# One token slot of a ViT tower on TensorE, its instruction order changed: scores together, turns together, fold and turned p later

## The chip, the cores and the metric

The kernel runs on one core of a Trainium2 chip. The metric is device time in microseconds (us), the median of several runs of the same program, lower is better. One more execution was recorded by the hardware profiler; its span, its busy times and its rows below come from that execution.

The engines are named as in the profile: PE is TensorE's matmul, PEld its weight load, DVE is VectorE, ACT is ScalarE, POOL is GpSimd, SP is SyncE, which issues most DMAs. Each engine runs its own instructions strictly in the written order and waits on semaphores.

## What is computed

A tower of three parts over 32 images of 256 x 64 x 64 (float32), cut to what matters:

```python
# tokenizer: 4x4 patches, one query per patch (the patch mean), keys and values from its 16 pixels
q    = LN(patch_mean) @ Wq.T
k, v = LN(pixels) @ Wkv.T
attn = softmax(q * scale . k)            # 8 heads, 16 pixels
h    = patch_mean + (attn . v) @ proj_w.T + proj_b
h    = concat([cls_tok, h])
# layer: a recurrence over the images (32 steps), then 8 experts, top 2
h = h + scan(tanh(LN(h) @ W_ih.T + b + hidden @ W_hh.T))
h = h + moe(LN(h))
```

## The kernel before, in words

The 8192 patches are worked in 64 units of 128 patches. `over_slots` (L91) writes out 66 slots, one after the other, without a loop on the chip. In slot k five units are in work at once: unit u = k is fetched and normalised (`front`), v = k-1 gets its attention scores and softmax (`mid`), w = k-2 its values and projection (`back`), z = k-3 the recurrence (`end`), and unit k-4 its routing (`late`). 61 slots, k = 3 to 63, have both `front` and `end`. After the slots come 86 expert tiles and the gather of the results, which the change does not touch.

Every engine has a function `slot` with its own written order; that order is what the change edits. Each helper is a few instructions with its waits ahead of it. On PE (L1040 to L1088), with the shape of the stationary tile (rows x columns of the array):

- 128x32: `means` (L883, patch means of u), `score` in two halves (L931, unit v), `fold_patches` (L948, v), `values` (L986, w).
- 128x128: `turn_z` 0 to 3 (L978, transposes of w), `turn_rn` (L897, u), `turn_xn` (L1005, z), `queries` (L904, u), `turn_tok` (L335), `recur` (L1013, z, float16), `turn_p` (L956, v), `project_out` (L998, w), `turn_h` (L1033, z), `logits` (L348), `turn_rs` (L925, u).
- 32x128: `project` (L913, u). 64x32: `weigh` (L961, v).

What joins the engines around the change:

- `means` of u; ACT `mean_out` writes rT (L725); DVE `mean_stats` (L1154), POOL `mean_scale` (L638), DVE `mean_norm` writes rn (L1169); PE `turn_rn`; ACT `rn_out` writes rnT; PE `queries`; ACT `q_out` writes qT (L736); PE `project`; ACT `u_out` (L744, four passes).
- `score` of v; DVE `unmask` writes sm (L1174); PE `fold_patches`; DVE `logits_in` (L1177, three steps); ACT `exps` (L756); DVE `total` and `divide`, which writes pr (L1198); PE `turn_p`; DVE `spread_p` writes pd (L1206); PE `weigh`.
- DVE `token_norm` writes xn of z (L1229); PE `turn_xn`; ACT `xn_out`; DVE `token_low` (L1232); PE `recur`; ACT `hidden` (L793); PE `turn_h`.
- `turn_z` of w; ACT `zT_out`; PE `values`; ACT `a_out`; PE `project_out`; DVE `token_stats`.
- DVE `stats` 0 to 7 of u, then `pixel_var` (L1148); POOL `pixel_scale` (L651); PE `turn_rs`; ACT `rep_out`; the next slot's `score`.

On SP the loads of pixels for unit k+2 go out in four parts of xp and four of xc, each behind a semaphore of PE (L577 to L606); `clear_rows` (L568) writes zeros behind `fold_patches`. xp has 4 buffers, xc has 3. From slot 43 on (`scatter_now`, L111) POOL also scatters two routed rows in each of 16 slots.

Of the kernel before, what the change touches and what calls it, by code (L numbers as in the profile page):

```python
# [72 lines left out]
def wait(eng, sem, unit, per, plus):  # L73

    v = unit.count(per, plus)
    if isinstance(v, int) and v <= 0:
        return
    eng.wait_ge(sem, v)
# [38 lines left out]
def vit_tower(nc, xc_in, xp_in, cls_tok, ln_q_w, ln_q_b, wqT, ln_kv_w, ln_kv_w_col, ln_kv_b, wk, wvT, projT, proj_b,  # L117
# [6 lines left out]
    with ctx:  # L124
# [123 lines left out]
        s = {n: sem(n) for n in names}  # L248
# [290 lines left out]
        @block.sync  # L539
        def _(sp):  # L540
            row_of = lambda a, n: a.partition_broadcast(n)
            for dst, src in ((spread[:, :], spread_in), (ident[:, :], ident_in)):
                sp.dma_start(dst, src).then_inc(s["first_in"], 16)
            load_xp(sp, 0, 0)
            loads = [(own[:, :], own_in), (cls_row[:, :], row_of(cls_tok, B)),
                     (fold[:, :], fold_in), (pick[:, :], pick_in),
                     (bih_c[:, :], b_ih), (bhh_c[:, :], b_hh),
                     (raw_ih, wihT.rearrange("(c p) n -> p c n", p=P)),
                     (raw_hh, whhT.rearrange("(c p) n -> p c n", p=P)),
                     (rw_s[:, :, :], routerT.rearrange("(c p) e -> p c e", p=P)),  # L550
                     (iota8[:, :], iota_in), (tri32, tri_in), (tile_no[:, :], tile_in[:, 0:NT]),
                     (before8[:, :, :], before_in.rearrange("p (a b) -> p a b", b=E))]
            assert len(loads) == NCONST
            for dst, src in loads:
                sp.dma_start(dst, src).then_inc(s["consts_in"], 16)
            sp.dma_start(b1_s[:, :, :], b1.rearrange("p (e c) -> p e c", e=E)).then_inc(s["consts_in"], 16)
            load_xc(sp, 0, 0)
            load_xp(sp, 1, 1)
            sp.wait_ge(s["w_ready"], 2)
            sp.wait_ge(s["rec_w"], 3)  # L560
            load_xc(sp, 1, 1)
            load_xp(sp, 2, 2)
            load_xc(sp, 2, 2)
            load_xp(sp, 3, 3)
            pieces = [(g, q, min(q + 3, 2 * TILES[g])) for g in GROUPS for q in range(0, 2 * TILES[g], 3)]
            sp.wait_ge(s["zero_set"], 1)

            def clear_rows(sp, n):  # L568

                g, q, e = pieces[n]  # L570
                sp.dma_start(xs_dram[g][q * P:e * P, :].rearrange("(k p) r -> p k r", p=P),
                             zero[:, :].unsqueeze(1).to_broadcast([P, e - q, C])).then_inc(clear[g], 16)

            def slot(sp, u, front, mid, back, end, late):
                v, w, t = u.before(), u.before(2), u.k - 4
                more_xp, more_xc = back and w.k + XBUF < UNITS, mid and v.k + XC < UNITS
                if more_xp:  # L577
                    wait(sp, s["z_ps"], w, 2, 2)
                    load_xp(sp, w.x, w.k + XBUF, [0])
                    wait(sp, s["rT_ps"], u, 1, 1)  # L580
                    load_xp(sp, w.x, w.k + XBUF, [1])
                    wait(sp, s["zt_ps"], w, 4, 2)
                    load_xp(sp, w.x, w.k + XBUF, [2])
                    wait(sp, s["rn_ps"], u, 1, 1)
                    load_xp(sp, w.x, w.k + XBUF, [3])
                for q in scatter_now(u.k)[1:]:
                    load_row(sp, q)
                if mid and 0 <= u.k - 2 < len(pieces):
                    wait(sp, s["c_ps"], v, 1, 1)
                    clear_rows(sp, u.k - 2)  # L590
                if more_xc:
                    wait(sp, s["s_ps"], v, 1, 1)
                    wait(sp, s["q_ps"], u, 1, 1)
                    load_xc(sp, v.c, v.k + XC, [0])
                if late:
                    keep_base(sp, t)
                    keep_row(sp, t)
                if more_xc:
                    if back:
                        wait(sp, s["a_ps"], w, 1, 1)  # L600
                    load_xc(sp, v.c, v.k + XC, [1])
                    wait(sp, s["u_ps"], u, 1, 1)
                    load_xc(sp, v.c, v.k + XC, [2])
                    if back:
                        wait(sp, s["pj_ps"], w, 1, 1)
                    load_xc(sp, v.c, v.k + XC, [3])  # L606
                for q in scatter_now(u.k + 1)[:1]:
                    load_row(sp, q)
                if u.k == UNITS - 1:
                    sp.wait_ge(s["s_ps"], UNITS - 2)  # L610
                    for e in range(E):
                        sp.dma_start(w1_in_s[:, e, :, :], w1[e].rearrange("(c p) n -> p c n", p=P)).then_inc(w1_in, 16)
                if u.k == UNITS:
                    sp.wait_ge(s["s_ps"], UNITS - 1)
                    for e in range(E):
                        sp.dma_start(w2_in_s[:, e, :, :], w2[e].rearrange("(c p) n -> p c n", p=P)).then_inc(w2_in, 16)
                if u.k == UNITS + 2:
                    sp.wait_ge(s["s_ps"], UNITS)
                    for q in range(RX):
                        sp.wait_ge(sent[q], 32 * len(range(q, SIZES[0], RX)))  # L620
                    for k in range(AHEAD):
                        load_tile(sp, 0, k, k)

            over_slots(sp, slot)
# [81 lines left out]
        def _(act):  # L706
# [107 lines left out]
            def slot(act, u, front, mid, back, end, late):  # L814
                v, w, z = u.before(), u.before(2), u.before(3)
# [8 lines left out]
                if back:  # L824
                    zT_out(act, w, 2)
                    zT_out(act, w, 3)
                if mid:
                    exps(act, v)
                if front:
                    q_out(act, u)  # L830
                if end:
                    xn_out(act, z)
                if back:
                    a_out(act, w)
                if front:
# [45 lines left out]
        def _(pe):  # L881
# [158 lines left out]
            def slot(pe, u, front, mid, back, end, late):  # L1040
                v, w, z = u.before(), u.before(2), u.before(3)
                if front:
                    means(pe, u)
                if mid:
                    score(pe, v, 0)
                if back:
                    turn_z(pe, w, 0)
                    turn_z(pe, w, 1)
                if mid:
                    score(pe, v, 1)  # L1050
                if back:
                    turn_z(pe, w, 2)
                if front:
                    turn_rn(pe, u)
                if back:
                    turn_z(pe, w, 3)
                if mid:
                    fold_patches(pe, v)
                if end:
                    turn_xn(pe, z)  # L1060
                if front:
                    queries(pe, u)
                if back:
                    values(pe, w)
                if front:
                    project(pe, u, back)
                if mid:
                    turn_p(pe, v)
                if late:
                    turn_tok(pe, u.k - 4, FB)  # L1070
                if end:
                    recur(pe, z, 0)
                    recur(pe, z, 1)
                if back:
                    project_out(pe, w)
                if end:
                    turn_h(pe, z)
                if late:
                    logits(pe, u.k - 4, FB)
                for g, part in pieces_now(u.k):  # L1080
                    if part == 4:
                        pe.wait_ge(s["lg_done"], u.k - 3)
                        route_ranks(pe, g, FB)
                if mid:
                    weigh(pe, v, front, 0)
                    weigh(pe, v, front, 1)
                if front:
                    turn_rs(pe, u)  # L1088
# [42 lines left out]
        def _(dve):  # L1131
# [128 lines left out]
            def slot(dve, u, front, mid, back, end, late):  # L1260
                v, w, z = u.before(), u.before(2), u.before(3)
# [12 lines left out]
                    route_norm(dve, u.k - 4)  # L1274
                if front:
                    stats(dve, u, [5])
                if mid:
                    logits_in(dve, v)
                if front:
                    stats(dve, u, [6])  # L1280
                if mid:
                    total(dve, v)
                    divide(dve, v)
                if end:
                    token_low(dve, z)
                if front:
                    stats(dve, u, [7])
                    pixel_var(dve, u)
                if mid:
                    spread_p(dve, v)  # L1290
# [408 lines left out]
```

## Time and profile before

| what | value |
|---|---|
| median of 3 runs | 1481.64 us (1477.16 to 1483.23) |
| span of the profiled execution | 1542.8 us |
| its PE, PEld, DVE, ACT, POOL busy | 87%, 69%, 69%, 54%, 46% |
| token slots (first to last `means`) | about 13 to 1095 us of the span |

For the profiled execution no time is listed besides its span; the span is 61 us (4%) above the median of the runs, so differences worked out inside the profile are taken off the median as they are. Busy is the time between an instruction's start and its modelled end; matmuls overlap, so the start of one group to the start of the next is what a group costs on PE. A bracket behind a row, as [0.25 <-ACT qT L736], is idle time ahead of it and what ended that idle time.

### The profile page before, as it was taken

To read this page: it belongs to the slowest core of one execution; us is meant where nothing else is said; L and a number is where in the kernel's file an instruction comes from. 1 tells how busy PE (TensorE), PEld (TensorE's weight loads), DVE (VectorE), ACT (ScalarE), POOL (GpSimd) and SP (SyncE) were. 2 spreads that over 40 slices of the span, in tenths; PEclk is the share of its full clock that TensorE was granted. 3 is DMA by queue.
4 is the path that set the end of the run, shared out by engine and by line. 5 is a ranking of instruction groups with operands and counts; after the bars stand their busy time and mean duration, and the time that the engine had idled before them with its cause. 6 is when DMAs were issued, how large, how long until landed. Compare 5 with 4: busy or idle time off the path is not lost. (4 is left out here: it accounts for less than half of the span.)

```text
span 1542.8 us, 63164 instructions
## 1 busy us (share of the span) xinstructions
PE 1342.3 (87%) x25681; PEld 1061.8 (69%) x25681; DVE 1067.5 (69%) x2855; ACT 832.4 (54%) x2065; POOL 711.1 (46%) x854
## 2 busy tenths in 40 slices
PE   4899999999999999999999999999959997688670
PEld 3677777777777777777776776677748896467550
DVE  4677777777777777878666666678756764467464
ACT  1455665655655655555555555555647774355340
POOL 2243343444434434343555555553313777552555
PEclk9999999999999999999999999999989998799795
DMA  7998898988998998988888989897245887687677
GB/s 259 407 307 298 293 308 297 305 295 295 310 297 276 314 293 280 294 278 293 303 309 302 300 306 312 296 313 256 71 153 193 272 283 245 186 267 255 207 232 227
DMA packets 186620, 423.78 MB, mean 275 GB/s; under 512 B 23968, under 2 KB 89312, under 8 KB 186208
## 3 DMA queue, kind: packets, MB, share of 16 engines
q1 hardware_dynamic: 170336, 380.27, 73.2%
q0 software_dynamic: 14048, 38.16, 7.8%
q8 instruction: 209, 3.42, 0.9%
q10 hardware_dynamic: 1952, 1.32, 0.3%
q14 instruction: 75, 0.61, 0.1%
HBM read 332.26 MB, written 87.39 MB: 272 GB/s over the span
## 5 line engine op out<-in xcount | busy, mean ns | idle before, releaser
L1146 DVE BATCH_NORM_STATS2 st<-xp 128x6 f32<-128x512 f32 x512 | 339.8, 695 | 16.4 <-DMA xp<-xpix 16.0
L656 POOL TENSOR_TENSOR rs_px<-px_ve,half_neg 128x16 f32<-128x16 f32 x64 | 187.0, 2922 | 179.9 <-DVE px_ve L1151 179.9
L770 ACT ACTIVATE zT<-bank 128x512 f32<-128x512 f32 x256 | 138.7, 597 | 75.3 <-PE bank L983 75.2
L1465 POOL DMA_INDIRECT y<-ys_dram,slot x130 | 126.3, 971 | 112.5 <-DVE fin L1628 47.1
L641 POOL TENSOR_TENSOR q_rs<-q_ve,half_neg 128x1 f32<-128x1 f32 x64 | 35.1, 549 | 289.7 <-DVE q_ve L1163 289.7
L763 ACT ACTIVATE z_s<-bank 128x512 f32<-128x512 f32 x256 | 138.6, 597 | 49.0 <-PE bank L973 49.0
L942 PE MATMUL bank<-xc,u 128*32 128x64 f32 x8192 | 149.4, 220 | 17.6 <-issue 17.0
L942 PEld LDWEIGHTS bank<-xc,u 128*32 128x32 f32 x8192 | 132.1, 110 | 41.3 <-issue 32.2
L893 PE MATMUL bank<-xp,spread 128*32 128x256 f32 x2048 | 140.4, 390 | 19.7 <-DMA xp<-xpix 13.4
L744 ACT ACTIVATE u<-bank 128x512 f32<-128x512 f32 x256 | 132.2, 602 | 41.5 <-PE bank L921 41.4
L983 PE MATMUL bank<-ident,z_s 128*128 128x128 f32 x1024 | 150.3, 279 | 1.9 <-issue 1.0
L415 POOL DMA_INDIRECT xs_dram<-xrow,slot x130 | 131.3, 1010 | 39.4 <-issue 34.8
L973 PE MATMUL bank<-xp,pd 64*32 64x256 f32 x4096 | 129.0, 382 | 3.2 <-ACT u L744 3.2
L1502 ACT ACTIVATE g<-bank,b_s 128x256 f32<-128x256 f32 x172 | 82.5, 480 | 82.5 <-PE bank L1552 41.4
L1615 DVE SCALAR_TENSOR_TENSOR y_s<-bank,b_rep 128x512 f32<-128x512 f32 x86 | 59.3, 690 | 94.3 <-remote 41.5
L983 PEld LDWEIGHTS bank<-ident,z_s 128*128 128x128 f32 x1024 | 111.6, 141 | 14.4 <-issue 1.6
L893 PEld LDWEIGHTS bank<-xp,spread 128*32 128x32 f32 x2048 | 64.9, 111 | 71.6 <-issue 37.2
L1158 DVE BATCH_NORM_STATS2 qst<-rT 128x6 f32<-128x256 f32 x64 | 27.2, 426 | 118.3 <-ACT rT L725 118.3
L1565 PE MATMUL bank<-xp,gh 128*128 x344 | 96.0, 279 | 12.1 <-issue 8.1
L1215 DVE TENSOR_TENSOR h_s<-bank,rc 128x256 f32<-128x256 f32 x64 | 27.2, 425 | 114.0 <-PE bank L1002 114.0
L1550 PE MATMUL bank<-xT,xp 128*128 128x256 f16 x344 | 96.4, 280 | 9.4 <-issue 9.3
L1551 PE MATMUL bank<-xT,xp 128*128 128x256 f16 x344 | 96.6, 281 | 7.9 <-issue 7.9
(195 smaller groups left out, 3398.5 us busy)
## 6 DMA issues: line engine op xcount, KB each, us to landing
xp<-xpix SPq DMA_DIRECT2D x256, 512.0 KB
xc<-xg SPq DMA_DIRECT2D x256, 512.0 KB
xc<-xs_dram SPq DMA_DIRECT2D x86, 256.0 KB
ys_dram<-y_s SPq DMA_DIRECT2D x86, 256.0 KB
xs_dram<-zero SPq DMA_DIRECT2D x57, 384.0 KB
base_dram<-h SPq DMA_DIRECT2D x65, 128.0 KB
rows_dram<-tok SPq DMA_DIRECT2D x65, 128.0 KB
hb<-base_dram SPq DMA_DIRECT2D x65, 128.0 KB
```

The source lines that it names most:

```text
L415: pool.indirect_dma_start(xs_dram[g], bass.IndirectOffsetOnAxis(ap=slot_u[k][0:n, t:t + 1], axis=0), xrow[i][0:n, :], None).then_inc(sent[ ...
L656: pool.tensor_tensor(rs_px[:, :], px_ve[:, :], half_neg[:, :], ALU.pow).then_inc(s["px_done"], 1)
L744: act.activation(uv[:, k, :, :, :], BIG[k][:, :].rearrange("p (m a t) -> p m a t", m=CC, t=TS), ACT.Copy).then_inc(s["u_done"], 1)
L763: act.activation(z_s[:, r, 2 * half:2 * half + 2, :].rearrange("p a c -> p (a c)"), BIG[2 * r + half][:, :], ACT.Copy).then_inc(s["z_done" ...
L770: act.activation(zT[:, c, :, :].rearrange("p h (a r t) -> p r h a t", r=2, t=TS)[:, r, :, :, :], BIG[f][:, :].rearrange("p (a h t) -> p h ...
L893: last = mm(FB[32 * k:32 * k + 32, 0:C], spread[:, 24 - 8 * q:56 - 8 * q], xp[u.x][:, 4 * k + q, :], start=(q == 0), stop=(q == 3))
L942: last = mm(SB[32 * k:32 * k + 32, (2 * n + r) * SUB:(2 * n + r + 1) * SUB], u_s[u.two][:, c, g, :, :].rearrange("p h t -> p (h t)"), xc[u ...
L973: last = mm(BIG[2 * r + half][32 * k:32 * k + 32, n * C:(n + 1) * C], pd[64 * r:64 * r + 64, g, :, :].rearrange("p h t -> p (h t)"), xp[v. ...
L983: last = pe.transpose(BIG[f][:, n * P:(n + 1) * P], z_s[:, r, n, c * P:(c + 1) * P], ident[:, :])
L1146: dve.bn_stats(st[:, j, :], xp[u.x][:, 2 * j:2 * j + 2, :].rearrange("p i c -> p c i")).then_inc(s["st_done"], 1)
L1465: pool.indirect_dma_start(y[q][0:n, :], None, ys_dram[g], bass.IndirectOffsetOnAxis(ap=slot_u[k][0:n, t:t + 1], axis=0)).then_inc(ga_in[q] ...
L1551: mm(o, wh, xl, start=False, stop=False)
```

## The change

Only the order of calls in `slot` changes, on four engines. No instruction is added or removed, and no wait is edited.

- PE: `score` 1 directly behind `score` 0; `turn_z` 0 to 2, `turn_rn`, `turn_z` 3, `turn_xn`, `queries` follow without a break; `fold_patches` goes from ahead of `turn_xn` to behind `queries`; `turn_p` goes from behind `project` to behind `recur`.
- ACT: `xn_out`, `q_out`, `exps` instead of `exps`, `q_out`, `xn_out`.
- DVE: `stats` 5 and 6 and `token_low` come ahead of `logits_in`, `stats` 7 ahead of `total` and `divide`.
- SP: `clear_rows` goes behind the first xc load.

```diff
@@ sync
                 for q in scatter_now(u.k)[1:]:
                     load_row(sp, q)
-                if mid and 0 <= u.k - 2 < len(pieces):
-                    wait(sp, s["c_ps"], v, 1, 1)
-                    clear_rows(sp, u.k - 2)
                 if more_xc:
                     wait(sp, s["s_ps"], v, 1, 1)
                     wait(sp, s["q_ps"], u, 1, 1)
                     load_xc(sp, v.c, v.k + XC, [0])
+                if mid and 0 <= u.k - 2 < len(pieces):
+                    wait(sp, s["c_ps"], v, 1, 1)
+                    clear_rows(sp, u.k - 2)
@@ scalar
+                if end:
+                    xn_out(act, z)
+                if front:
+                    q_out(act, u)
                 if mid:
                     exps(act, v)
-                if front:
-                    q_out(act, u)
-                if end:
-                    xn_out(act, z)
@@ tensor
                 if mid:
                     score(pe, v, 0)
+                    score(pe, v, 1)
                 if back:
                     turn_z(pe, w, 0)
                     turn_z(pe, w, 1)
-                if mid:
-                    score(pe, v, 1)
-                if back:
                     turn_z(pe, w, 2)
                 if front:
                     turn_rn(pe, u)
                 if back:
                     turn_z(pe, w, 3)
-                if mid:
-                    fold_patches(pe, v)
                 if end:
                     turn_xn(pe, z)
                 if front:
                     queries(pe, u)
+                if mid:
+                    fold_patches(pe, v)
                 if back:
                     values(pe, w)
                 if front:
                     project(pe, u, back)
-                if mid:
-                    turn_p(pe, v)
                 if late:
                     turn_tok(pe, u.k - 4, FB)
                 if end:
                     recur(pe, z, 0)
                     recur(pe, z, 1)
+                if mid:
+                    turn_p(pe, v)
                 if back:
                     project_out(pe, w)
@@ vector
                 if front:
                     stats(dve, u, [5])
+                    stats(dve, u, [6])
+                if end:
+                    token_low(dve, z)
                 if mid:
                     logits_in(dve, v)
                 if front:
-                    stats(dve, u, [6])
+                    stats(dve, u, [7])
                 if mid:
                     total(dve, v)
                     divide(dve, v)
-                if end:
-                    token_low(dve, z)
                 if front:
-                    stats(dve, u, [7])
                     pixel_var(dve, u)
```

## Rows read from the trace of the kernel before

**Rows 1.** Stages: width, busy time (count) of PE, PEld, DVE, ACT, POOL, clock, DMA share, GB/s

```profile
1131.80:1135.10 3.30, 3.30 (x40) 2.85 (x33) 0.40 (x1) 0.77 (x2) 0.69 (x1) 0.50 0.24 79
100.00:1095.00 995.00, 941.33 (x21062) 731.42 (x21059) 737.33 (x2151) 575.52 (x1457) 452.00 (x555) 1.00 0.88 293
```

**Rows 2.** Timeline of PE, 401 to 437 us: start, length, line, tiles, shapes, count [idle before]

```profile
410.72 1.93 PE L893 MATMUL bank<-xp,spread 128*32 128x256 f32 x32
412.47 1.08 PE L942 MATMUL bank<-xc,u 128*32 128x64 f32 x64
413.47 1.09 PE L983 MATMUL bank<-ident,z_s 128*128 128x128 f32 x8
414.50 1.10 PE L942 MATMUL bank<-xc,u 128*32 128x64 f32 x64
415.53 0.66 PE L983 MATMUL bank<-ident,z_s 128*128 128x128 f32 x4
416.02 0.38 PE L901 MATMUL bank<-ident,rn 128*128 128x128 f32 x2
...
416.98 0.43 PE L952 MATMUL bank<-sm,pick 128*32 128x128 f32 x8
417.33 0.44 PE L1010 MATMUL bank<-ident,xn 128*128 128x128 f32 x2
417.61 1.06 PE L909 MATMUL bank<-rnT,wq_s 128*128 128x128 f32 x8
418.60 1.08 PE L994 MATMUL bank<-zT,wv_s 128*32 128x128 f32 x32
419.93 1.17 PE L921 MATMUL bank<-qT,wk_s 32*128 32x128 f32 x32 [0.25 <-ACT qT L736]
421.03 0.33 PE L959 MATMUL bank<-ident,pr 128*128 128x128 f32 x1
...
422.77 1.08 PE L1002 MATMUL bank<-pj_s,aT 128*128 128x256 f32 x4
...
424.79 1.96 PE L973 MATMUL bank<-xp,pd 64*32 64x256 f32 x64
...
426.94 1.93 PE L893 MATMUL bank<-xp,spread 128*32 128x256 f32 x32
...
432.23 0.38 PE L942 MATMUL bank<-xc,u 128*32 128x64 f32 x10 [0.53 <-issue]
...
434.42 1.06 PE L909 MATMUL bank<-rnT,wq_s 128*128 128x128 f32 x8
...
436.42 0.84 PE L921 MATMUL bank<-qT,wk_s 32*128 32x128 f32 x20
```

**Rows 3.** Timeline of PE inside one `score`, 413.19 to 413.31 us

```profile
412.98 0.55 PE L942 MATMUL bank<-xc,u 128*32 128x64 f32 x24
```

**Rows 4.** Timeline of DVE, 404 to 424 us

```profile
413.20 0.43 DVE L1158 BATCH_NORM_STATS2 qst<-rT 128x6 f32<-128x256 f32 x1 [1.71 <-ACT rT L725]
...
415.19 0.40 DVE L1169 TENSOR_SCALAR rn<-rT,qmv,q_rs 128x256 f32<-128x256 f32 x1
...
416.24 0.68 DVE L1174 TENSOR_TENSOR sm<-bank,fold 128x512 f32<-128x512 f32 x1
416.84 0.40 DVE L1229 TENSOR_SCALAR xn<-h_s,hmv,h_rs 128x256 f32<-128x256 f32 x1
...
420.09 0.29 DVE L1198 TENSOR_TENSOR pr<-ex,rden 128x128 f32<-128x128 f32 x1
```

**Rows 5.** Timeline of ACT, 404 to 424 us

```profile
419.05 0.31 ACT L756 ACTIVATE ex<-sc 128x128 f32<-128x128 f32 x1 [1.25 <-DVE sc L1185]
419.27 0.61 ACT L736 ACTIVATE qT<-bank,qb_col 128x128 f32<-128x128 f32 x2
```

**Rows 6.** Waits of all engines, 100 to 1095 us: total, times, longest

```profile
PE bank L942 <- issue: 13.4, 17, 1.5
PE bank L1037 <- ACT hT L793: 12.0, 58, 0.2
```

## The prediction, made before the changed kernel ran

> **What bounds the kernel now.** I read the busy time by stages first. Between 100 and 1095 us, which is nearly the whole token part, PE is busy 941 of 995 us at a clock of 1.00, DVE 737, ACT 576, and the DMA engines 0.88 of the time [rows 1]. PE sets the pace there, and DMA is near behind it. The change touches the token slots alone, so the experts after them are left as they are.
>
> Then the timeline of PE over one slot. A quiet slot is 16.22 us (410.72 to 426.94, start of `means` to start of the next), and groups follow each other almost without a gap [rows 2]. The reader should look at two things. First, what a change of tile shape costs. Inside a score, 24 matmuls start within 0.33 us, so four of them (one per column strip) take 0.056 us [rows 3]; 64 would take 0.89, but the first score holds PE for 1.00 and the second for 1.03 [rows 2]: 0.11 is lost on leaving for the transposes and 0.03 on coming in from them. A transpose is 0.11 (two in 0.22, 416.02 to 416.24, where L983 goes on behind the two of L901); four behind a score take 0.49 rather than 0.44, and eight take 1.03 rather than 0.93 with both ends in it. So a trip from 128x32 to 128x128 and back costs 0.11 + 0.05 + 0.10 + 0.03 = 0.29 us. Second, where PE waits for others: `project` stands 0.25 for qT, and `fold_patches` starts 0.06 behind the end of sm (416.24 + 0.68 = 416.92, then 416.98) [rows 2, 4], so it waits for DVE as well.
>
> Then the timeline of DVE, because PE's waits end there. DVE stands 1.71 us for rT at 413.20 and from there works without a break through rn, the routing statistics, sm and xn; xn ends at 416.84 + 0.40 = 417.24, that is 6.52 us behind the start of `means` [rows 4]. This chain hangs on `means` and on DVE's own order, and the change leaves DVE's order up to xn as it is.
>
> **The change part by part.**
>
> PE, first half of the slot. Two round trips go: the one between the score halves, and the one around the fold, which now sits between `queries` and `values` where PE changes shape anyway. That is 2 x 0.29 = 0.58 us of PE's time a slot. How much of it is seen? In the new order PE reaches `turn_xn` at: 1.75 (`means`) + 2 x 0.89 + 0.11 (scores) + 0.05 + 18 x 0.11 (16 `turn_z`, 2 `turn_rn`) = 5.67 us behind `means`, and on the way reaches `turn_rn` at about 5.0, when rn is there (415.59, 4.87). But xn comes at 6.52. With the 0.06 that the fold needed behind sm, `turn_xn` starts at 6.58, and PE stands 0.9 us. In the old order it started at 417.33, 6.61. So the first half gives 0.03, not 0.58: the fold was what PE did while DVE made xn, and what is late next is xn. Of score halves moved earlier nothing is gained on DVE either: sm started at 416.24 because DVE was busy until then, not because the scores were late.
>
> PE, `turn_xn` to `project`. Old: `queries` at 6.89, `project` at 9.21. Where `project` does not stand for qT, it starts 2.00 behind `queries` (434.42 to 436.42 in the next slot) [rows 2]. New: `queries` 0.28 behind `turn_xn`, at 6.86; the fold adds two steps of 0.11 and no trip, so `project` can start at 6.86 + 2.00 + 0.22 = 9.08.
>
> ACT. `q_out` stood behind `exps`, and `exps` stood 1.25 us for DVE; that made qT late (419.88) [rows 5]. With `q_out` first, it starts when `queries` end, about 1.06 behind their start, at 7.95, and lasts 0.61: qT at 8.56, 0.5 ahead of `project`. So the 0.25 goes, and PE's own work is the bound to `project`: 9.21 - 9.08 = 0.13 us a slot.
>
> `exps` behind `q_out`, fold later. The fold starts at 6.86 + 0.99 = 7.85 instead of 6.26. Old: pr was done 3.40 behind the fold's start (420.38 against 416.98). With the same 3.40, though `stats` 6 and `token_low` no longer stand in that stretch but ahead of it, pr comes at 11.25. `turn_p` is wanted behind `recur`: `project` 9.08 + 1.10 (419.93 to 421.03) + 1.57 (421.03 to 422.77 without the 0.17 of `turn_p`) = 11.75. Cover 0.5; if it is gone, `turn_p` stands with `project_out`, `turn_h` and `weigh` behind it. `turn_p` to `weigh` is then 2.2 us rather than 3.76; `spread_p` between them is a pass of the size of sm, 0.68, so it has room.
>
> `turn_p` moved. PE does the same work between `project` and `turn_h` in either order, and `turn_h` stands for hT 0.2 us in 58 slots of 58 [rows 6]; hT hangs on ACT's `u_out`, which starts at the end of `project`. So this move is worth nothing, and it does no harm while the 0.5 holds.
>
> DVE's other moves (`stats`, `token_low`) keep the sum of its work up to `pixel_var`, so I cost them at nothing; their cover is the 1.71 that DVE stands in each slot. `pixel_var` now follows `divide`, so pr at 11.25 is its bound too; POOL's `pixel_scale` and, at the slot's end, `turn_rs` hang on it. POOL's own order isn't edited, and its scatters wait for tok, which DVE makes right behind xn as before.
>
> SP. The third xp part waits for `turn_z` 1, now behind the second score, about 0.9 later; the fourth hardly moves; `clear_rows` lets the first xc part by and then holds the row stores and the other xc parts until the fold's end, up to 0.4 later than before. These loads are for a unit used at least a slot later, and the DMA share would go from 0.88 to about 0.89. Cost taken: nothing; bounds 0 and 0.1 a slot.
>
> Stalls inside the scores. PE stands there 13.4 us in 17 stalls, up to 1.5, with nothing named as the cause [rows 6]. The old order pays for part: in the slot of 426.94 with a 0.53 stall, `project` starts 9.48 behind `means`, 0.27 late [rows 2]. The new order has 0.9 us of standing at `turn_xn` behind it, and a stall of up to that size costs nothing. I take a quarter of a us for each of the 17, 4 us; bounds 0 (they move to another place) and 10.
>
> **Sum.** 61 slots x 0.13 = 8, and 4 from the stalls: 12 us. The durations are those of an execution whose span is 1542.8, 61 us above the median; I take the same 12 us off the median: 1481.6 - 12 = 1470 us.
>
> **A rule that speaks against it.** Rows first: the clock is 1.00 from 100 to 1095, and fell to 0.50 in 1131.80 to 1135.10, in the slots that run out, where PE stands for us at a time [rows 1]. The new order makes one run of 18 transposes, a stand of 0.9 and two more: 3 us, where the longest before is 1.4 (415.53 to 416.98). No row of before shows a slot like that. The Trainium skill, TensorE: Matmul & The Clock Gate, Part 4 (PE-mode transpose), says that a transpose doesn't count as PE being busy in the way that a matmul does for the clock. By it the new run could look idle and the clock could fall in each slot; by the rows it does not.
>
> **The rivals.**
>
> *Clock falls.* The place is the run of turns. If each of 61 slots had a stretch such as that of 1131.80 (3.3 us at 0.50, so 1.65 lost), it would be 61 x 1.65 - 12 = +89: 1570 us. For: nothing in the rows; against: 2.9 us is mixed with scores ahead and `queries` behind. Chance 0.04.
>
> *Slower: scores outrun their supply.* The stalls in the scores are there now, and 128 short matmuls in one go, with their weight loads, ask for instructions faster than any other stretch. If each slot stalled as in the 17, by 1.2 us, `turn_xn` would start at 5.67 + 1.20 = 6.87, 0.29 behind the forecast's, and the slot would lose 0.16 against before: 61 x 0.16 = 10, 1491 us. It decides from a stall of 0.9 + 0.13 = 1.04 us a slot. Against: only 17 stalls in 61 slots now. Chance 0.08.
>
> *Nothing that can be measured.* The stalls move to places without cover, and the 16 slots with scatters, where POOL and its transfers set more of the pace, give nothing: 45 x 0.13 = 6, 1476 us. With a few tenths lost where `exps` comes late in those slots, 1480. Chance 0.26.
>
> *All of it shows.* If xn were no bound, `project` would start at 5.67 + 0.22 + 2.00 + 0.22 = 8.11, 1.10 earlier, 61 x 1.10 = 67: 1415 us. Against it stands the DVE chain above. Chance 0.05.
>
> **How the numbers follow.** The forecast has 0.57; its own range is 1462 (stalls at their upper bound, and the waits of the first and last slots with them) to 1473 (no stall saved). A measurement of this kernel tells 0.5% (7.4 us) from no change. Faster: 0.57 + 0.05 = 0.62; same 0.26; slower 0.08 + 0.04 = 0.12. The range takes in the forecast and the no-change case and leaves out the rest: 1460 to 1483.
>
> **What would show it.** Right: a quiet slot of 16.09 us; `turn_xn` 6.58 behind `means` with a wait of about 0.9 named for xn; no wait of `project` for qT; the wait of `turn_h` for hT still 0.2; fold directly behind `queries`. Wrong: a slot under 15.9 (then xn was not the bound), waits at `turn_p` for pr or at `weigh` for pd, stalls in the scores in most slots, or a clock under 1.00 between 100 and 1095.

## The result, and the profile after

The change makes the kernel **slower by 1.2%**: median 1494.58 us (1484.51 to 1503.86, 20 runs) against 1477.06 (1463.92 to 1489.39, 20 runs) for the kernel before in the same comparison, ratio 1.0118, interval 1.0097 to 1.0138. The forecast was 1470 us, range 1460 to 1483. The profiled execution of the changed kernel took 1503.86 us, 9 above its median; its span is 1502.2.

A quiet slot is as forecast. The timeline of PE over the slot that starts at 454.69 us (start, length, engine, line, tiles, shapes, count, idle time ahead with its releaser), against [rows 2]:

```profile
454.69 1.93 PE L893 MATMUL bank<-xp,spread 128*32 128x256 f32 x32
456.44 1.97 PE L942 MATMUL bank<-xc,u 128*32 128x64 f32 x128
458.34 1.53 PE L983 MATMUL bank<-ident,z_s 128*128 128x128 f32 x12
...
461.27 0.44 PE L1010 MATMUL bank<-ident,xn 128*128 128x128 f32 x2 [0.71 <-DVE xn L1227]
461.54 1.06 PE L909 MATMUL bank<-rnT,wq_s 128*128 128x128 f32 x8
462.53 0.43 PE L952 MATMUL bank<-sm,pick 128*32 128x128 f32 x8
...
463.76 1.18 PE L921 MATMUL bank<-qT,wk_s 32*128 32x128 f32 x32
...
466.49 0.28 PE L959 MATMUL bank<-ident,pr 128*128 128x128 f32 x1
...
467.90 0.44 PE L1037 MATMUL bank<-ident,hT 128*128 128x128 f32 x2 [0.27 <-ACT hT L793]
...
470.76 0.42 PE L893 MATMUL bank<-xp,spread 128*32 128x256 f32 x4
```

The slot lasts 16.07 us (470.76 - 454.69; 16.09 was forecast, 16.22 is the slot of [rows 2]). `turn_xn` starts 6.58 behind `means`, with a wait for xn (0.71 idle); `project` at 9.07 (9.08 forecast) without a wait for qT; `turn_p` at 11.80 (11.75); `turn_h` still stands for hT.

The loss is in the slots that are not quiet. The timeline of the slot behind 417.05 us:

```profile
417.05 1.94 PE L893 MATMUL bank<-xp,spread 128*32 128x256 f32 x32
418.80 1.73 PE L942 MATMUL bank<-xc,u 128*32 128x64 f32 x109
423.47 0.53 PE L942 MATMUL bank<-xc,u 128*32 128x64 f32 x19 [2.94 <-issue]
423.93 1.53 PE L983 MATMUL bank<-ident,z_s 128*128 128x128 f32 x12
...
435.47 1.94 PE L893 MATMUL bank<-xp,spread 128*32 128x256 f32 x32
```

PE stands 2.94 us in the middle of the second score, and the profile names no semaphore: "issue". It is not a single case. PE's waits from 100 to 1095 us (us in total, times, longest), against [rows 6]:

```profile
PE bank L942 <- issue: 63.2, 44, 3.1
PE bank L1037 <- ACT hT L793: 14.8, 58, 0.3
PE bank L983 <- issue: 9.5, 5, 2.7
PE bank L1010 <- DVE xn L1227: 6.7, 12, 0.8
```

The scores' issue stalls went from 13.4 us in 17 to 63.2 in 44, with 9.5 more in `turn_z`. The stages of the same kernel (width, busy time and count of PE, PEld, DVE, ACT, POOL, granted clock, DMA share, GB/s), the first against [rows 1]:

```profile
100.00:1095.00 995.00, 898.24 (x20980) 734.59 (x20973) 737.98 (x2148) 578.39 (x1450) 449.23 (x555) 0.98 0.85 293
...
303.00:306.00 3.00, 0.16 (x7) 0.09 (x8) 1.98 (x7) 0.00 (x0) 1.65 (x3) 0.97 0.61 231
306.00:309.50 3.50, 3.50 (x30) 3.33 (x30) 2.56 (x5) 1.19 (x2) 0.73 (x1) 0.54 0.10 18
309.50:313.00 3.50, 3.50 (x75) 3.13 (x77) 1.67 (x5) 2.68 (x8) 0.00 (x0) 1.00 0.90 280
```

The clock is down from 1.00 to 0.98 as a mean. In the second row PE stands in a stall (0.16 us busy of 3.00); in the row behind it the granted clock is 0.54, nearly the level of 1.2 GHz, and in the fourth row it is back at that of 2.4. So a long stall can be paid twice. There are nine such falls from 100 to 1095 us, each within 1.2 us of the end of a stall of 2.1 to 3.1 us. Not every such stall has one: of 14 over 2.0 us five have none, that of 2.94 us above among them. The slot with the fall of these rows has nearly the same stall:

```profile
299.47 1.93 PE L893 MATMUL bank<-xp,spread 128*32 128x256 f32 x32
...
305.90 0.65 PE L942 MATMUL bank<-xc,u 128*32 128x64 f32 x14 [2.84 <-issue]
306.49 2.82 PE L983 MATMUL bank<-ident,z_s 128*128 128x128 f32 x12
...
319.35 1.93 PE L893 MATMUL bank<-xp,spread 128*32 128x256 f32 x32
```

Its 12 turns take 2.82 us rather than 1.53, and it lasts 19.88 us where the slot of 417.05 lasts 18.42 at a clock of 1.00. So the stall costs some 2.4 us against a quiet slot, and the fall about 1.4 more. What sets stalls with a fall apart from those without one, no run here shows.

**Where the time went.** The profile of before that the prediction used was of an unusually long execution, so the kernel before was recorded again:

> The kernel before, unchanged, for a second profile: the first one had a span 61 us above the median of the runs. Theory (instruction supply): the stalls in the scores add to 25 to 45 us between 100 and 1095 us when the slots with scatters run without the pauses of the first profile, all of them at page borders; quiet slots 16.2 us; span 1470 to 1490 us. Rival: 13 us as in the first profile.

It took 1468.7 us. Its waits of PE, and then its stage from 100 to 1095 us:

```profile
PE bank L942 <- issue: 24.4, 30, 2.0
PE bank L1037 <- ACT hT L793: 12.6, 59, 0.2
PE bank L921 <- ACT qT L736: 6.5, 26, 0.3
```

```profile
100.00:1095.00 995.00, 938.88 (x21560) 738.75 (x21552) 753.46 (x2200) 589.61 (x1490) 458.57 (x565) 1.00 0.87 295
```

Slot by slot (start of `means` to the next, 59 slots from k = 4 to 62), each kernel's time above its own quiet slot, and in brackets the stalls of over 0.3 us in it (here and in the tables of experiment 3 a stall counts from the start of the last matmul ahead of it, some 0.2 us more than the profile's idle time):

```
                                  after              before again
quiet slot                        16.06              16.21
slots with a fall of the clock    9: +31.5 (25.0)     1: + 3.6 ( 2.2)
other slots with a stall         41: +32.7 (60.6)    33: +20.9 (34.0)
slots without                     9: + 2.6           25: + 8.1
sum                                  +66.7              +32.5
```

59 x 0.15 = 9 us are gained on quiet slots, 66.7 - 32.5 = 34 are lost on the others: 25 us more in the token part. 27.9 of the lost time lie in slots with a fall of the clock, 11.8 in slots with a stall alone, and 5.5 are gained on the rest. Of the 27.9 the falls themselves are some 11 by the pair above (8 more falls x 1.4, an estimate); the rest is the length of their stalls. The medians are only 17.5 apart, because the two recorded executions lie on opposite sides of their medians; the expert stage behind the slots, 404 us against 395, is not touched by the change. The split is that of one execution each: in the first record of before, that of [rows 1], the same 59 slots took 1013.0 us, against 989.1 in the second and 1014.4 in the changed kernel. So the loss itself rests on the medians and on the experiments below.

### The profile page after: what moved, and what is told of

Read it like the earlier page. It is cut to its first block and busy times, and to the rows that moved or that the text cites. A ratio compares the mean times of both kernels' runs of the same rounds, so it can differ in the third digit from the quotient of the medians.

```text
span 1502.2 us, 63164 instructions
## 1 busy us (share of the span) xinstructions
PE 1288.1 (86%) x25681; PEld 1063.9 (71%) x25681; DVE 1069.2 (71%) x2855; ACT 841.7 (56%) x2065; POOL 711.1 (47%) x854
## 3 DMA queue, kind: packets, MB, share of 16 engines
q8 instruction: 209, 3.42, 0.9%
## 5 line engine op out<-in xcount | busy, mean ns | idle before, releaser
L1144 DVE BATCH_NORM_STATS2 st<-xp 128x6 f32<-128x512 f32 x512 | 333.6, 694 | 15.3 <-DMA xp<-xpix 14.8
L942 PE MATMUL bank<-xc,u 128*32 128x64 f32 x8192 | 140.4, 221 | 66.8 <-issue 66.3
L942 PEld LDWEIGHTS bank<-xc,u 128*32 128x32 f32 x8192 | 130.6, 111 | 85.1 <-issue 74.4
L893 PE MATMUL bank<-xp,spread 128*32 128x256 f32 x2048 | 127.2, 390 | 17.8 <-DMA xp<-xpix 13.1
L983 PEld LDWEIGHTS bank<-ident,z_s 128*128 128x128 f32 x1024 | 122.1, 149 | 19.7 <-issue 13.0
L1204 DVE TENSOR_TENSOR pd<-bank,rs_own 128x512 f32<-128x512 f32 x64 | 44.3, 692 | 87.1 <-PE bank L959 87.1
L893 PEld LDWEIGHTS bank<-xp,spread 128*32 128x32 f32 x2048 | 61.8, 111 | 59.3 <-issue 20.6
L1548 PE MATMUL bank<-xT,xp 128*128 128x256 f16 x344 | 94.9, 276 | 0.4 <-ACT gh L1500 0.4
L1549 PE MATMUL bank<-xT,xp 128*128 128x256 f16 x344 | 94.9, 276 | 0.0
```

What stands on the lines that cost most here:

```text
L893: last = mm(FB[32 * k:32 * k + 32, 0:C], spread[:, 24 - 8 * q:56 - 8 * q], xp[u.x][:, 4 * k + q, :], start=(q == 0), stop=(q == 3))
L942: last = mm(SB[32 * k:32 * k + 32, (2 * n + r) * SUB:(2 * n + r + 1) * SUB], u_s[u.two][:, c, g, :, :].rearrange("p h t -> p (h t)"), xc[u ...
L983: last = pe.transpose(BIG[f][:, n * P:(n + 1) * P], z_s[:, r, n, c * P:(c + 1) * P], ident[:, :])
L1144: dve.bn_stats(st[:, j, :], xp[u.x][:, 2 * j:2 * j + 2, :].rearrange("p i c -> p c i")).then_inc(s["st_done"], 1)
L1548: mm(o, wh, xh, start=(c == 0), stop=False)
```

## The experiments

L942 is the scores' line in all that follow, except where said. "Stall" is an issue stall of PE.

**1. Which call does it?** The first four kernels ran on one chip beside the same runs of the kernel before. The changed kernel with score 1 put back:

```diff
 score(pe, v, 0)
-score(pe, v, 1)
 turn_z(pe, w, 0)
 turn_z(pe, w, 1)
+score(pe, v, 1)
 turn_z(pe, w, 2)
```

> The changed kernel with one part undone: score 1 stands behind turn_z 1 again, everything else of the change stays. Theory (instruction supply): the stalls in the scores come from 256 PE instructions issued in one go, a whole page of instructions, faster than the next page can be fetched. Then the stalls here fall back from 66 us to 10 to 25 us, the quiet slot stays at 16.07 us because turn_xn waits for xn at 6.58 us either way, and the time is 1462 to 1472 us, ratio 0.990 to 0.997. Rival (the other moves: fold, turned p, q_out ahead of exps, the SP order, make the loss): the stalls stay at 50 us or more, ratio 1.005 to 1.015. Rival (clock falls in the run of turns): the runs of turns around turn_xn with its wait are still there, so the clock still falls in places between 100 and 1095 us, ratio over 1.00.

Measured 1473.3 us (1462.04 to 1483.27), ratio 0.9975 (0.9949 to 1.0001). The loss is gone, but less of the stalls than expected: 38.9 us are left rather than 10 to 25, and the clock still falls four times. And the other way round, the kernel before with nothing but score 1 moved forward (the same diff reversed):

> The kernel before with one part of the change alone: score 1 directly behind score 0. Theory (instruction supply): the stalls in the scores come up to 50 us or more, quiet slots stay near 16.2 us since fold_patches waits for sm as before, ratio 1.010 to 1.025. Rival (the other moves make the loss): stalls under 25 us and a ratio of 0.99 to 1.00.

Measured 1489.46 us, ratio 1.0075 (1.0048 to 1.0102): stalls as expected, the ratio a little under the 1.010 expected. PE's waits of the first, then of the second:

```profile
PE bank L942 <- issue: 38.9, 35, 2.7
PE bank L1010 <- DVE xn L1229: 9.0, 19, 0.8
```

```profile
PE bank L942 <- issue: 55.5, 43, 3.2
```

The adjacent scores alone cost 11 us (0.75%), and without them the rest of the change is at most a small gain. So the whole loss hangs on the place of one call.

**2. Was xn the bound?** The changed kernel with DVE's `token_norm` ahead of the routing statistics and `unmask`, and then the same with score 1 put back as above:

```diff
 mean_norm(dve, u)
+token_norm(dve, z)
 ...
-token_norm(dve, z)
```

> The changed kernel with DVE's token_norm (xn) moved ahead of route_stats and unmask. If turn_xn's wait for xn is what hid the saved shape changes, the quiet slot goes from 16.07 to 15.2 to 15.4 us (turn_xn at 5.67 us instead of 6.58). The page stalls then have no cover and show in full, so the whole gains less than 61 x 0.8: time 1455 to 1485 us, ratio 0.985 to 1.005. Rival (xn is not the bound, PE is): the quiet slot stays at 16.0 to 16.1 us.

Measured 1491.06 us, ratio 1.0096 (1.0063 to 1.0128), above the time expected.

> Both: scores apart and xn made first. Theory: turn_xn can start at 5.96 us (one more change of shape than in the changed kernel), quiet slot 15.4 to 15.6 us, stalls in the scores 10 to 35 us, time 1430 to 1450 us, ratio 0.97 to 0.98. Rival (DMA becomes the bound at 0.92 busy): slots spread above 16 us with PE waiting for xp or xc, ratio 0.985 or more.

Measured 1467.41 us (1461.21 to 1475.13), ratio 0.9927 (0.9899 to 0.9954): **faster than both kernels**, 0.7% below the kernel before where 2 to 3% were expected. The rival of this run, DMA as the bound, doesn't show: the list of PE's waits has none for xp or xc, and the DMA share from 100 to 1095 us is 0.87. This kernel's waits of PE, and then the timeline of a quiet slot:

```profile
PE bank L942 <- issue: 37.6, 38, 2.0
PE bank L1037 <- ACT hT L793: 18.1, 59, 0.8
```

```profile
400.83 1.93 PE L893 MATMUL bank<-xp,spread 128*32 128x256 f32 x32
...
406.79 0.38 PE L1010 MATMUL bank<-ident,xn 128*128 128x128 f32 x2
...
413.64 0.44 PE L1037 MATMUL bank<-ident,hT 128*128 128x128 f32 x2 [0.44 <-ACT hT L793]
...
416.50 0.42 PE L893 MATMUL bank<-xp,spread 128*32 128x256 f32 x4
```

In both, `turn_xn` waits for nothing and the quiet slot falls from 16.07 to 15.67 us (416.50 - 400.83): xn was the bound, and hT is next, which keeps the slot above the 15.2 to 15.6 expected. But of 59 x 0.40 = 24 us hardly any is seen with the scores adjacent, where the ratio is 1.0096 instead of the 1.0118 of the changed kernel: what stood idle for xn had been covering stalls. With the scores apart there is less to cover, and half a per cent shows (0.9975 to 0.9927, intervals that just touch). The kernel with both edits is called the fourth kernel from here on.

**3. What is "issue"?** All stalls of the changed kernel (47 of over 0.3 us idle from 100 to 1095 us) stop at the same place when PE's instructions are counted in 256s (all records of matmuls, weight loads and PE's sequencer, from the start of the program). Some of them, read out of the trace, with the end of the last 16 KB transfer of the "instruction" queue ahead of the restart:

```
line  stands from-to      us    instruction mod 256   transfer landed   to restart
L942  302.84-305.91     3.06    193                   304.59            1.31
L942  420.32-423.47     3.16    194                   422.13            1.34
L983  729.57-732.54     2.97    194                   731.24            1.29
L942  955.07-958.25     3.18    194                   956.87            1.38
```

The page's line of that queue (transfers, MB, share):

```profile
q8 instruction: 209, 3.42, 0.9%
```

That is 3.42 MB / 209 = 16.4 KB a transfer, and the trace has 53514 instructions of PE: 256 a transfer. PE works through its instructions in blocks of 256 (the expectations call them pages), and a block comes while the one ahead of it is used. In the trace such a transfer starts 2.4 us (median; 1.2 to 3.9 for eight in ten) behind PE's step into the block ahead, takes 1.0, and the first instruction of the new block runs 1.4 behind its landing. Together some 4.8 us, so what decides most is how long 256 instructions last. 160 blocks of the token part, by how long the block ahead lasted (blocks, stalled ones, us of their stalls, those over 0.35 us; the last column is experiment 5):

```
block ahead lasted    after              before again       scores far apart
under 3.5 us          24, 24, 50.5       14, 11, 12.8        0,  0,  0
3.5 to 4.0            17, 17, 22.6       14,  9,  6.4       12,  6,  6.2
4.0 to 4.5            14, 12, 14.6       22, 13, 15.4       31, 19, 21.8
4.5 to 5.0             9,  0,  0         15,  4,  2.2       21,  3,  3.4
over 5.0              96,  4,  2.5       95,  6,  4.3       96, 15, 12.4
```

A score is 64 matmuls and 64 weight loads; the two together are a whole block, used in 1.9 us. A slot has 733 instructions, so the borders wander by 35 a slot (768 - 733), and every slot is hit in another place. The table has no sharp limit: in the last column 15 of 96 blocks stall behind one that lasted over 5.0 us.

**4. The test: same work, borders elsewhere.** If so, the position of the borders alone must decide. The fourth kernel with 35 instructions that wait on a long-reached semaphore added to a slot (768 instructions, three blocks), and a number of such waits ahead of the first slot that puts the borders into one place for good. Two waits of the text make one instruction (24 + 24 + 22 = 70 for 35); slots 4 to 63 are filled but for 40 and 41, and from 42 on `more` takes one instruction off. The two kernels differ in the number ahead only:

```diff
+def fill(pe, n):
+    for _ in range(n):
+        pe.wait_ge(s["first_in"], 32)
...
+fill(pe, 24)
 recur(pe, z, 0)
 recur(pe, z, 1)
+fill(pe, 24)
 turn_p(pe, v)
 project_out(pe, w)
+fill(pe, 22 + more)
 turn_h(pe, z)
...
+fill(pe, 244)   # 36 in e6_pages_uneven
 means(pe, first)
```

> The kernel of e4 with filling only: 35 PE instructions that wait on a semaphore long reached are written into each of the slots 4 to 63, so that a slot is 768 = 3 x 256 instructions, and 122 more ahead of the first matmul. With 733 a slot, the borders of the 256-instruction pages wander through the slot; with 768 they stand still, here at instruction 228 of the slot (in the first score), the others in values and in weigh, so that the three pages take about 4.9, 6.0 and 4.7 us. Theory (instruction supply: a page is asked for when the one before it begins to be used, and is there 3.5 to 6.3 us later): stalls of 0.8 us a slot on average instead of 1.1 to 1.3, between 25 and 50 us in all, and none at other places; time 1435 to 1465 us, ratio 0.97 to 0.99. Rival (the stalls are of the scores, not of the pages, for example from reading xc): the stalls stay as in e4 and lie wherever a score is; the filling costs up to 1 us a slot.

Measured 1479.68 us, ratio 1.003 (1.0004 to 1.0055): above the time expected.

> The same instructions and the same filling in the slots as in e5, with 18 filling instructions ahead of the first matmul instead of 122. The page borders then stand at instruction 76 of each slot (at the start of the first score) and one page holds both scores: the pages take about 2.8, 6.5 and 6.3 us. Theory (instruction supply): about 2 us of stall in every slot, 100 to 130 us in all, nearly all at one instruction, behind the second score; time 1510 to 1560 us, ratio 1.02 to 1.055. Rival (the stalls are of the scores or of the data): the time is that of e5 within 5 us, since the work, its order and the number of instructions in a slot are the same.

Measured 1539.4 us, ratio 1.0424 (1.0381 to 1.0468). PE's waits of the first, then of the second, and in the timeline of the second one of its stalls:

```profile
PE bank L1023 <- issue: 23.5, 58, 0.5
PE bank L973 <- issue: 7.1, 13, 1.4
PE bank L959 <- issue: 6.0, 36, 0.2
PE bank L942 <- issue: 3.6, 7, 1.1
```

```profile
PE bank L942 <- issue: 65.1, 55, 3.1
PE bank L1023 <- issue: 19.5, 53, 0.4
```

```profile
893.43 0.30 PE L942 MATMUL bank<-xc,u 128*32 128x64 f32 x2 [2.74 <-issue]
```

60 us between two kernels with the same slots, by 104 instructions that do nothing, ahead of the first: the scores' stalls are 3.6 us in one and 65.1 in the other, there almost in every slot and two matmuls ahead of the end of score 1. This shows the cause: where the borders lie. The stalls of the second come to less than the 100 to 130 us expected; its time is in the range because the filling costs, too. The time expected of the first was missed, because the filling itself isn't free: PE idles 0.4 us at L1023 in each filled slot (23.5 us, 58 times), the quiet slot is 16.02 rather than 15.67, and that eats what is saved.

Can filling be hidden? First between the recurrence's matmuls, one by one:

```diff
 mm(o, hh_h[:, c, w], hT_h[z.two][:, c, 0:n], start=(c == 0), stop=False)
+if filled:
+    fill(pe, 2)
```

> As e5_pages_even (768 instructions a slot, page borders at the same three places), but 24 of the 35 filling instructions stand one by one between the 24 matmuls of the recurrence, which follow each other every 57 ns, in place of 12 in a row ahead of it and 12 behind it; the other 11 stay ahead of turn_h. In e5_pages_even TensorE idles 0.47 us behind the 12 ahead of the recurrence and 0.17 us behind the next 12, and its quiet slot is 16.02 us where e4_apart_xn_first has 15.67; its stalls on instructions are 21 us from 100 to 1095 us against some 60 there, so it loses by filling about what it gains by even pages. Theory (pages of 256 instructions, each of which has to last some 4.7 us, set the stalls; filling costs only where TensorE has nothing else to do): the filling between matmuls is hidden, the quiet slot comes down to 15.67 to 15.8, the scores' issue stalls stay under 12 us, and the time is 1450 to 1466 us, ratio 0.982 to 0.994 to the kernel before. Rival (each filling instruction costs its 14 to 39 ns wherever it stands): quiet slot 16.0 or longer, time 1474 to 1490, ratio 0.998 to 1.01.

Measured 1480.28 us, ratio 1.0049 (1.0021 to 1.0077), with a quiet slot of 16.22 us: the rival. Only the scores' stalls came down as the theory had it (3.7 us). The timeline shows what a row of waits does:

```profile
414.87 0.22 PE L1044 MATMUL bank<-xnT_l,ih_h 128*128 128x129 f16 x1
414.92 0.22 PE L1038 MATMUL bank<-xnT_h,ih_h 128*128 128x129 f16 x1
415.01 0.22 PE L1041 MATMUL bank<-xnT_h,ih_l 128*128 128x129 f16 x1
415.13 0.22 PE L1044 MATMUL bank<-xnT_l,ih_h 128*128 128x129 f16 x1
...
415.44 0.22 PE L1031 MATMUL bank<-hT_l,hh_h 128*128 128x129 f16 x1
415.57 0.22 PE L1034 MATMUL bank<-hT_h,hh_l 128*128 128x129 f16 x1
```

Up to the tenth matmul (the one at 414.92) they follow at 0.06 us, behind it mostly at 0.12 to 0.13. It looks as if PE's sequencer were ahead of the array at first and the waits used that up; no row shows the sequencer's lead itself. Then the 35 spread, nine in the queries, nine in the recurrence, six in `project_out`, eleven ahead of `turn_h`:

> As e8_pages_between (768 instructions a slot, the same page borders but for a few instructions), with the 35 filling instructions spread: 9 between the four matmuls of the queries (three at a time), 9 behind the first nine matmuls of the recurrence, 6 between the two of project_out, 11 ahead of turn_h. In e8_pages_between the first nine of the 24 between the recurrence's matmuls cost nothing (the matmuls follow at 57 ns), and each one from the tenth on takes its matmul to 125 ns. Theory (TensorE's sequencer runs some tenths of a us ahead of the matmuls, and filling is hidden as long as it stays ahead; even pages then give what they save): quiet slot 15.67 to 15.85 us, issue stalls from 100 to 1095 us about 20 us as there, time 1455 to 1469 us, ratio 0.985 to 0.996 to the kernel before. Rival (the filling cannot be hidden, or the page that is shortest comes out shorter): quiet slot 16.0 or more, or stalls of over 35 us, time 1474 to 1490.

Measured 1468.73 us, ratio 0.9937 (0.9903 to 0.9972); the quiet slot is 15.84. So spreading takes half of the first filling's price away (0.17 us a slot above the fourth kernel instead of 0.35), and the time is at the upper end of what was expected, but no better than that of the unfilled fourth kernel.

**5. Longer blocks by order alone.** The fourth kernel with score 1 behind all four `turn_z`:

```diff
 turn_z(pe, w, 0)
 turn_z(pe, w, 1)
-score(pe, v, 1)
 turn_z(pe, w, 2)
-turn_rn(pe, u)
 turn_z(pe, w, 3)
+turn_rn(pe, u)
+score(pe, v, 1)
 turn_xn(pe, z)
```

> As e4_apart_xn_first (733 or 734 instructions a slot, no filling, the same number of changes of shape), but score 1 stands behind all four turn_z and turn_rn, directly ahead of turn_xn: 2.3 us of turns between the two scores instead of 1.0, where e3_xn_first has none. Theory (a page of 256 instructions has to last some 4.7 us): the shortest 256 instructions of a slot last 3.8 us instead of 2.8 (2.0 with none between), and the mean shortfall of a page, worked out over all positions of the borders in the quiet slot of e4_apart_xn_first, falls from 1.16 to 0.98 us a slot (1.46 with none between): the longest stall falls from 2.0 to under 1.5 us, the sum of the issue stalls from 100 to 1095 us by some 5 to 12 us, quiet slot 15.65 to 15.8, time 1457 to 1467, ratio 0.985 to 0.993 to the kernel before. Rival (the score's own matmuls are what stalls, wherever they stand): stalls as in e4_apart_xn_first, up to 2 us long, ratio 0.992 or more; a later sm (its end 6.9 behind means instead of 6.5) may then show as a wait of the fold or of turn_p.

Measured 1469.19 us, ratio 0.9952 (0.9922 to 0.9981). PE's waits:

```profile
PE bank L1037 <- ACT hT L793: 28.4, 57, 0.6
PE bank L942 <- issue: 20.9, 22, 1.7
PE bank L901 <- DVE rn L1167: 9.4, 33, 1.1
```

The scores' stalls fall, in sum by more than expected, the longest by less: with 0, 1.0 and 2.3 us of turns between the scores (the third, the fourth and this kernel) they are 60.6, 37.6 and 20.9 us, the longest 3.2, 2.0 and 1.7. No fall of the clock is left in the token slots. But the time is above what was expected and not below the fourth kernel's: PE now waits for rn and longer for hT, and the quiet slot is 16.12, which was not foreseen. One term was bought with another.

## Why the prediction was wrong

**Right: every step on a quiet slot.** xn as the bound of the first half, so that 0.58 us of trips give 0.03 (confirmed by the third and fourth kernels, where 0.40 more comes free once xn is early, until hT is the bound); the wait for qT gone; `turn_p` covered; the 0.13 a slot (0.15 measured, 16.21 to 16.06). SP's loads were costed at nothing, and no wait for them stands in the list of PE's waits.

**Wrong: the step "Stalls inside the scores".** It took the 17 stalls as given, asked only whether they would be covered, and booked 4 us as a gain, bounds 0 and 10, both on the good side. The cover was judged about rightly: 41 slots with 60.6 us of stalls cost 32.7, so 0.7 us a slot were covered where 0.9 had been taken. What failed was that the new order makes stalls. It packs 256 instructions into 1.9 us where a block needs some 4.8 to come, so they grew to 63.2 us in 44 (17 and 13.4 in [rows 6], 30 and 24.4 in the second record of before), up to 3.1 us long against a cover of 0.9.

**The rival "scores outrun their supply" was right** in place and mechanism. That its 1491 us lie near the 1494.58 measured is luck: it took a stall of 1.2 us "as in the 17", whose mean is 0.8 (13.4 / 17, [rows 6]), put it into each of 61 slots, and left out the clock; the runs show stalls in most slots but not in all (50 of 59), longer ones, and nine falls. It was held down to 0.08 by "only 17 stalls in 61 slots now", which speaks of the order in which turns stood between the scores.

**The rival "clock falls"** fell at the wrong place. In quiet slots the run of 18 turns leaves the clock at 1.00 (454.69 to 470.76). It fell behind stalls, where PE had done nothing for 2.1 to 3.1 us. The Trainium skill, TensorE: Matmul & The Clock Gate, Part 4 (PE-mode transpose), by which a transpose doesn't count as PE being busy in the same way, finds no support in these slots: in the last kernel 18 turns stand between the scores too, and its token slots have no fall at all.

**The cause beside a rule.** The stalls stand where a block of 256 instructions begins, behind transfers of 16.4 KB. The Trainium skill, Runtime: NRT & Kernel Launch, Instruction fetch mechanics, says that instructions come in blocks of 16 KiB (256 instructions), fetched by the sequencer's own DMA queue; with that the trace agrees. It also says that the cost of a border is "mostly hidden". Here it isn't: 63.2 us in one line.

**Open.** Why a transfer starts 1.2 us behind the border in one case and 3.9 in another was not tried; the DMA engines are 0.85 busy meanwhile. Nor was a score with fewer, larger instructions. Why only nine of the 14 long stalls brought the clock down is open, too.

## What to carry to other kernels

An idle gap marked "issue" inside a row of short matmuls is a cost with a cause: count the instructions in the stretch and how long it lasts, and keep short-instruction stretches apart (here most blocks of 256 that lasted under 4.5 us were followed by a stall). Before sorting work by kind to save changes of mode, ask what the mixing paid for: long instructions between short ones give the supply time. And a gain on the quiet slot is only worth what the disturbed slots leave of it, so bound a stall on the side of getting worse, too.

## What was not expected of the hardware

- Two kernels that differ by 104 empty instructions ahead of the first slot are 60 us (4%) apart.
- A stall on instructions can bring the clock down to 0.5 behind it: nine of the changed kernel's 14 stalls over 2.0 us did. With stalls of 2.84 and 2.94 us, the slot with a fall took 3.8 us more than a quiet one and the slot without it 2.4.
- Of added waits that are long fulfilled, one behind each matmul of the recurrence, the first nine cost PE nothing and the later ones about 0.07 us each (0.057 to 0.125 from matmul to matmul).
